# Two context attentions of a four-layer decoder: probabilities of the last one turned by DMA, one GpSimd step of the masked one moved

## The reference, cut to what matters

```python
q = rmsnorm((hidden_states @ Wq).reshape(B, Sq, H, D), gq)
k = rmsnorm((encoder_hidden_states @ Wk).reshape(B, Skv, H, D), gk)
v = (encoder_hidden_states @ Wv).reshape(B, Skv, H, D)
scores = einsum('bqhd,bkhd->bhqk', q, k) / sqrt(D)
attn = softmax(scores, axis=-1)
out = einsum('bhqk,bkhd->bqhd', attn, v).reshape(B, Sq, H * D)
return out @ Wo
```

## Time and profile before

| what | value |
|---|---|
| median of 3 runs | 3162.02 us |
| the profiled execution | 3164.6 us, span 3162.8 us |
| `l1x`: its scores, first to last | 747.1 to 1033.6 us |
| `l3x`: its scores, first to last | 2498.7 to 2896.2 us |
| busy share of the whole span | PE 88%, DVE 69%, ACT 60%, POOL 56% |
| mean granted TensorE clock | 0.947 |

### The profile page before, as it was taken

The page is one execution under the profiler, slowest core; times in us unless marked ns, Lnnn a source line. Parts: engine busy times, 40 slices in busy tenths (PEclk is TensorE's granted clock), DMA queues, the critical chain, the costliest instruction groups (busy, mean ns, idle before and its releaser), DMA issues. The chain is left out here.

```text
span 3162.8 us, 71599 instructions
## 1 busy us (share of the span) xinstructions
PE 2777.2 (88%) x25387; PEld 2136.6 (68%) x25483; DVE 2175.5 (69%) x5175; ACT 1898.9 (60%) x3885; POOL 1785.5 (56%) x1904
## 2 busy tenths in 40 slices
PE   7969999798999785895787999899999799998998
PEld 5757775466777564674565555688888677776565
DVE  5567764546777523884786677677777577787787
ACT  3346763355777331564786555566666599996675
POOL 2122211224888465554883376688888599897800
PEclk9999999799999876997999999899999999999999
DMA  4010001001333554000002532000000000001000
GB/s 166 1 24 14 12 10 67 7 1 32 67 65 62 156 129 90 6 6 22 16 18 80 194 86 69 3 1 0 0 0 0 8 7 5 5 5 60 11 1 28
DMA packets 162524, 121.42 MB, mean 38 GB/s; under 512 B 108076, under 2 KB 149484, under 8 KB 159343
## 3 DMA queue, kind: packets, MB, share of 16 engines
q1 hardware_dynamic: 157688, 112.89, 12.7%
q0 software_dynamic: 4608, 5.57, 1.1%
HBM read 80.85 MB, written 13.71 MB: 30 GB/s over the span
## 5 line engine op out<-in xcount | busy, mean ns | idle before, releaser
L2232 PE MATMUL bank<-l3a_ln_xnT,far 128*128 128x128 f16 x3072 | 194.4, 220 | 1.8 <-POOL l3a_ln_xnT L2046 1.8
L2232 PEld LDWEIGHTS bank<-l3a_ln_xnT,far 128*128 128x128 f16 x3072 | 181.7, 99 | 3.3 <-POOL l3a_ln_xnT L2046 2.2
L877 PE MATMUL bank<-l2f_xnT,l2f_wi 128*128 128x512 f16 x672 | 157.2, 383 | 7.0 <-POOLq L741 6.4
L3616 PE MATMUL bank<-l0x_v,l0x_pT 128*128 128x128 f32 x1024 | 133.9, 279 | 4.1 <-ACT l0x_pT L4045 2.5
L3616 PEld LDWEIGHTS bank<-l0x_v,l0x_pT 128*128 128x128 f32 x1024 | 126.8, 191 | 14.9 <-issue 5.8
L1226 PE MATMUL bank<-l3f_xnT,near 128*128 128x512 f16 x480 | 120.4, 388 | 7.3 <-DVE l3f_xnT L1011 3.9
L1241 PE MATMUL bank<-near,l3f_h 128*128 128x256 f16 x960 | 119.1, 274 | 6.0 <-DVE l3f_h L1016 2.6
L877 PEld LDWEIGHTS bank<-l2f_xnT,l2f_wi 128*128 128x128 f16 x672 | 65.4, 99 | 78.3 <-POOLq L741 9.9
L1241 PEld LDWEIGHTS bank<-near,l3f_h 128*128 128x128 f16 x960 | 94.0, 98 | 35.2 <-DVE l3f_h L1016 4.2
L3102 ACT ACTIVATE l3x_prob<-bank,l3x_less,l3x_q_rr 128x128 f32<-128x128 f32 x256 | 114.1, 459 | 3.0 <-DVE l3x_less L2981 3.0
L2836 PE MATMUL bank<-l1x_ln_xnT,far 128*128 128x128 f16 x1536 | 96.3, 219 | 18.3 <-POOL l1x_ln_xnT L2046 15.0
(11 more groups left out here) (735 smaller groups left out, 9312.5 us busy)
## 6 DMA issues: line engine op xcount, KB each, us to landing
far<-in_l1f_in SPq DMA_DIRECT2D x32, 256.0 KB, 3.7
l2f_front<-l2f_shares SPq DMA_DIRECT2D x5, 1024.0 KB, 4.5
sums<-near SPq DMA_DIRECT2D x2, 2176.0 KB, 19.2
far<-in_l1f_down SPq DMA_DIRECT2D x32, 128.0 KB, 4.2
far<-sums SPq DMA_DIRECT2D x8, 512.0 KB, 7.3
l2f_wi<-in_l2f_in SPq DMA_DIRECT2D x14, 256.0 KB, 6.3
far<-l0x_kT SPq DMA_DIRECT2D x64, 48.0 KB
far<-l2x_kT SPq DMA_DIRECT2D x32, 96.0 KB
```

Source lines behind the costliest of these rows:

```text
L877: last = nc.tensor.matmul(bank[:, :], wi16[n % 2][p][:, a, k, :], xnT[q][:, k, 512 * g:512 * g + 512], start=(k + p + q == 0), stop=(k == ...
L2232: last = nc.tensor.matmul(bank[:, P * j:P * j + P], w(k, 512 * c + P * j, P, p), norm.xnT[u][q][:, k, :], start=(k + p + q == 0), stop=(k ...
L3616: last = nc.tensor.matmul(b_o[:, at:at + P], pT[f % 3][:, j, :], v_all[b % NV][:, hv:hv + P], start=True, stop=True)
```

## The change

In `l3x`:

- The four exponentials write to PSUM bank 6 and not to `prob` in SBUF.
- VectorE's `sums` takes the reciprocal, drains, and multiplies bank 6 by it into `prob` (SBUF).
- ScalarE's `upper_probs` and GpSimd's `lower_probs` split `prob` into `p16`; SyncE turns both halves by one DMA transpose into `pT`, as in `l1x`.
- Gone are PE's `turn_probs`, DVE's and ACT's `keep_probs`, and GpSimd's `divide`.
- SyncE runs the row of slots, so the context's load is issued in slot (b, 0), and `heads_out` waits for the DMA.

In `l1x`: GpSimd's `norm.second_half` of chunk 2 stands first in its slot, ahead of `lower_probs`, and not behind `split_q`.

```diff
-        b_p, b_kT = (core.bank[6:8], None) if merged else (core.bank[6:7] * 2, core.bank[7])
+        b_p, b_kT = core.bank[6:8]
@@ sync
-                if merged:
-                    run_slots(sp, slot, NC, 2, K_O)
-                    return
-                with sp.Fori(1, NB // 2) as i:
-                    for u in range(2):
-                        sp.wait_ge(c_split, 2 * i + u - 1)
-                        load(2 * i + u, u)
+                run_slots(sp, slot, NC, 2, K_O)
@@ tensor
                 def heads_out(it):
                     b, u, c_, f = it
-                    if merged:
-                        pe.wait_ge(p_turned[c_ % 2], turns(b, c_) + 16)
-                    else:
-                        pe.wait_ge(pT_lo, f + 1)
+                    pe.wait_ge(p_turned[c_ % 2], turns(b, c_) + 16)
...
                         if sc:
                             scores(sc)
-                        if pr:
-                            turn_probs(pr)
@@ vector, sums
-                    nc.vector.reciprocal(srec[c_ % 2][:, :], ssum[c_ % 2][:, :]).then_inc(sum_ready, 1)
+                        nc.vector.reciprocal(srec[c_ % 2][:, :], ssum[c_ % 2][:, :]).then_inc(sum_ready, 1)
+                        return
+                    nc.vector.reciprocal(srec[c_ % 2][:, :], ssum[c_ % 2][:, :])
+                    dve.drain()
+                    since(dve, p_split, f - 1)
+                    nc.vector.tensor_tensor(heads(prob[c_ % 2][:, :]), heads(b_p[:, :]),
+                                            srec[c_ % 2][:, :].unsqueeze(2).to_broadcast(wide), ALU.mult
+                                            ).then_inc(p_ready, 1)
@@ vector, slot
-                        if pr:
-                            keep_probs(pr)
@@ scalar, exponentials
-                    since(act, p_split if merged else p_turned, f - 1)
+                    since(act, *((p_split, f - 1) if merged else (p_ready, f)))
...
-                        last = nc.scalar.activation(prob[c_ % 2][:, at], b_s[:, at], ACT.Exp,
+                        last = nc.scalar.activation(b_p[:, at], b_s[:, at], ACT.Exp,
@@ scalar, slot
                         if pr:
-                            keep_probs(pr)
+                            upper_probs(pr)
@@ gpsimd, slot
                     if merged:
+                        if ln and c_ == 2:
+                            norm.second_half(pool, b, u)
                         if pr:
                             lower_probs(pr)
...
-                        if ex:
-                            divide(ex)
+                        if pr:
+                            lower_probs(pr)
                         if kk:
                             key_rsqrt(kk)
...
-                    if merged and ln and c_ == 2:
-                        norm.second_half(pool, b, u)
```

More of the change, by code:

```diff
@@ L2664, in context_attention_layer @@
         qT = [two(f"qT{u}", 512, F16) for u in range(2)]
-        if merged:
[L2666 to L2670, removed]
-        else:
-            pT = [two(f"pT{u}", 512, F16) for u in range(2)]
-            p_turned, pT_hi, pT_lo = sem("p_turned"), sem("pT_hi"), sem("pT_lo")
+        p16 = [sb(f"p16{u}", [P, 2 * HC, P], F16) for u in range(2)]
+        pT = [sb(f"pT{u}", [P, 2 * HC, P], F16) for u in range(2)]
+        p_hi, p_split, p_cleared = sem("p_hi"), sem("p_split"), sem("p_cleared")
+        c_freed = sem("c_freed")
+        p_turned = [sem(f"p_turned{u}") for u in range(2)]
         oT = [two(f"oT{u}", 512, F16) for u in range(2)]
@@ L2767, in merge @@
                         last.then_inc(m_made, 1)
[L2769 to L2776, removed]
                 def squares(it):
@@ L2850, in heads_out @@
                     for p, q in HALVES:
-                        turned = pT[c_ % 2][:, HC * q:HC * q + HC, :].rearrange("p h k -> p (h k)") if merged else (
-                            pT[c_ % 2][q][:, :])
-                        last = nc.tensor.matmul(b_o[:, :], c16[u][p][:, :], turned,
+                        last = nc.tensor.matmul(b_o[:, :], c16[u][p][:, :],
+                                                pT[c_ % 2][:, HC * q:HC * q + HC, :].rearrange("p h k -> p (h k)"),
                                                 start=(p + q == 0), stop=(p == 1))
@@ L3004, in keep_keys @@
                                                    ALU.mult, ALU.subtract).then_inc(kT_lo, 1)
[L3006 to L3010, removed]
                 def residual(b):
@@ L3124, in upper_probs @@
                     nc.scalar.copy(p16[c_ % 2][:, 0:HC, :], heads(prob[c_ % 2][:, :])).then_inc(p_hi, 1)
[L3126 to L3130, removed]
                 def keep_q(it):
```

## The result

| | before | changed |
|---|---|---|
| median of 12 runs each | 3161.59 us | 3152.76 us |
| lowest and highest | 3156.71, 3168.45 | 3145.91, 3156.81 |
| the profiled execution | 3164.6, span 3162.8 | 3150.5, span 3148.7 |

The ratio is 0.997, with a 95% interval of 0.9962 to 0.9978: 9 us faster, 7 to 12. The forecast was 14 faster, 3148 us.

What follows compares the result with a forecast made beforehand. No engine alone was the bound; PE's waits inside slots, through GpSimd's queue, were. l1x -18 and l3x +4 gave -14 on 3164.6 us, 3150.6; with the median 2.6 lower, 3148 us, range 3134 to 3161.

Steps and rivals of the forecast that it cites:

- l1x, -18: In l1x, PE's query projection stops waiting for GpSimd's moved second_half; 1.24 us saved a batch, 18 in all, bounds 15 to 19.
- the hole: In l1x, GpSimd idles 0.89 us before lower_probs, waiting for ScalarE; the moved step needs 0.67 of it, delaying nothing.
- l3x, the mechanism: In l3x, transposes leave PE, but heads_out waits about 0.6 us every other slot for GpSimd's lower_probs and a 3.25 us DMA trip.
- both halves of the chain: In l3x, heads_out to heads_out over two slots: chunk 1 to 3 takes 12.50 us, chunk 3 to 1 takes 12.45.
- l3x, +4: Sum for l3x: -0.8 from steady batches, +1.9 stage end, +1 filling the pipe, +1.6 small terms; 4 us slower.
- 24.95 us a batch: In l3x, predicted steady batch length along the path through lower_probs and the DMA, against 25.0 before the change.
- +0.1 for jitter: In l3x, allowance per batch for small terms that could not be placed, 1.6 us over the stage.
- The ends of the stage, +1.9 and +1: In l3x, last reciprocal to last heads_out grows from 4.15 to 6.07 us, +1.9; filling the pipe costs an estimated +1.
- Exponential into PSUM: In l3x, ScalarE's exponential taken at 0.46 us, bounds 0.42 and 0.48; four on the chain, -3 or +1 us.
- A: The forecast itself: l1x gives 15 to 19 us, l3x costs up to 9 or gives up to 3; chance 0.57.
- B: In l3x the DMA trip is hidden and PE's wait for divide gone: l3x -12, in all -30, 3132 us; chance 0.15.
- D: In l3x, heads_out pays 3.2 us per 0.1 us of longer trip: l3x +26, in all +8, 3170 us; chance 0.06.

## Why the prediction was off by 5 us

- **l1x, -18**: right. 17 measured alone, and the mechanism as told: the hole, no follow-up, PE the bound.
- **l3x, the mechanism**: right, though not the whole of what the order of GpSimd is worth. The transposes' room on PE is taken up by heads_out waiting for a trip, in every second slot, and both halves of the chain go through query_rsqrt and lower_probs. Two trips a batch are shown by the delayed trip, and the way out by the order of GpSimd.
- **l3x, +4**: the term that was mis-sized. It measures 11 alone and 8 within the change (3152.76 against 3145.03 with the move alone); in the traces, 7.6 alone. The forecast's 24.95 us a batch, 25.05 with its jitter, is 25.32. Of the 0.37 over 24.95, the two trips make 0.2 (3.27 to 3.40 for 3.25). The rest are places where I took distances of the old timeline though a new step stands there, and they show in every other batch: in the one above scores start 2.10 us after heads_out (2713.65 to 2715.75) and not 1.95, because keep_keys stands behind the multiply, and from heads_out to the next one with no wait for a DMA it is 5.42 (2700.88 to 2706.30), not 5.25, because project_k waits for the scaled keys; in the next batch these are 1.97 and 5.34. The "+0.1 for jitter" was a guess in place of these two terms.
- **The ends of the stage, +1.9 and +1**: the last reciprocal at 2883.10 and the last heads_out at 2889.17 are 6.07 us apart, exactly the sum. Filling the pipe cost 1.3, near the 1 that I had guessed: the first four batches take 107.0 us with l3x's part alone and 105.7 before. But the last three slots take 17.9 us there in place of 16.1, since two of them now hold a wait for a trip, and I had costed only the very last trip. In the change they take 19.1; PE's clock makes the difference, below.
- **Exponential into PSUM**: taken at 0.46, measured 0.427; the bounds held it. But the starts stay 0.44 us apart, so it could not pay four times on the chain, as its bounds had it. That its place matters through GpSimd was not seen.
- **Rivals**: A held for l1x, while l3x's cost is at the edge of its "up to 9" or past it (the interval alone is 7 to 16). B (hidden trip, 3132) is what the kernel with lower_probs first shows, at 3133; the change did not get there. D's price, 3.2 us for 0.1 of trip, is about right: 1.30 us cost 48 us, 3.7 for each 0.1, the falls of the clock included.

## What to carry to other kernels

Before a step is moved from TensorE to a DMA, walk the chain through the queue that feeds the DMA: what counts is not the load of the engines but how long the producer's input has been lying there. An in-order engine's wait for something else is a free place for a step that is ready; lower_probs ahead of two steps took 20 us off, where the whole rewrite had taken off 9. And split a change into its parts on the chip: this one was a gain of 17 us that carried a loss of 11.

## What was not expected of the hardware

- A GpSimd instruction and a VectorE multiply with both inputs in SBUF hold each other up: 1.45 us for 1.01, 1.02 for 0.69. With one input of the multiply in PSUM the multiply is never longer. A VectorE step of 128x4 elements with its input in SBUF (`l3x_k_var`) takes 0.17 us, and up to 0.6 where lower_probs is running, until that ends.
- TensorE's granted clock fell at the stage's end, after PE had stood waiting for trips. The changed kernel's end, then the end before:

```profile
2876.00:2880.00 4.00, 4.00 (x27) 2.62 (x25) 1.53 (x3) 2.05 (x5) 2.49 (x3) 0.61 0.35 65
...
2888.00:2892.00 4.00, 2.83 (x12) 1.67 (x13) 0.69 (x1) 0.59 (x1) 0.00 (x0) 0.67 0.16 29
```

```profile
2896.00:2900.00 4.00, 2.73 (x27) 2.01 (x24) 2.77 (x7) 2.88 (x10) 0.42 (x1) 1.00 0.00 0
2900.00:2904.00 4.00, 3.39 (x25) 2.18 (x23) 1.83 (x3) 1.17 (x2) 0.62 (x1) 1.00 0.00 0
```

  A mean of 0.61 is part 2.4 and part 1.2 GHz. Before the second fall PE had stood 2.26 us, and three matmuls of 512 columns then took 1.29 us in place of 0.82, as the timeline of the changed kernel's end has it, with the last reciprocal ahead of it:

```profile
2883.10 0.18 DVE L2935 RECIPROCAL l3x_srec<-l3x_ssum 128x4 f32<-128x4 f32 x1 [1.01 <-ACT bank L3076]
...
2889.17 1.29 PE L2829 MATMUL bank<-l3x_pT,l3x_c 128*128 128x512 f16 x3 [2.26 <-DMA l3x_pT<-l3x_p]
```

  Standing for so long is not enough for it: with l3x's part alone PE stands as long at the same place, and the clock stays at 1.00 there, as the timeline and the busy time by stretch of that kernel have it:

```profile
2917.64 0.82 PE L2829 MATMUL bank<-l3x_pT,l3x_c 128*128 128x512 f16 x3 [2.27 <-DMA l3x_pT<-l3x_p]
```

```profile
2916.00:2920.00 4.00, 2.26 (x17) 1.51 (x18) 0.69 (x1) 0.58 (x1) 0.00 (x0) 1.00 0.29 54
```

  The two kernels have the same l3x, so their difference prices the falls: 1.2 us of the change's last three slots (19.1 against 17.9), and 1.0 in the last output projection (4.03 against 3.05). What decides whether the clock falls stays open.
- A transpose of half the size is issued in almost the same time on SyncE (1.19 and 1.24 us) and its matmuls start 0.54 us sooner.
